# Attention: TensorE takes two key steps at a time

## The chip, the cores and the metric

The kernel runs on one core of a Trainium2 chip. What counts is the device time of one launch in microseconds (us). Three runs of the kernel before gave a median of 2147.2 us (2143.27 to 2149.08).

## The reference

One transformer block over x of shape 4 x 1024 x 512 in float32: a layer norm with scale and shift, attention with 16 heads of size 32, a gated residual, then a second norm and a mixture of 16 experts (two for each token) beside a shared feed-forward. Only the attention concerns us:

```python
kqv = (x @ Wqkv + bqkv).reshape(b, s, 3, NUM_HEADS, HEAD_SIZE)
q, k, v = kqv[:, :, 0], kqv[:, :, 1], kqv[:, :, 2]
scores = jnp.einsum('bsnh,btnh->bnst', k, q) / math.sqrt(HEAD_SIZE)
scores = jnp.triu(scores) + -10000.0 * jnp.tril(ones, k=-1)
attn = jax.nn.softmax(scores, axis=2)
out = jnp.einsum('bnkq,bknh->bqnh', attn, v)
```

The softmax runs over keys, and a query sees the keys up to itself. Each of the four batches has 1024 positions.

## The kernel before

Each engine has its own program, written out by hand, and waits on semaphores. An instruction whose semaphore is not there yet holds up everything behind it on its engine.

`attention_phase` treats a batch at a time, and in it eight pairs of heads, p = 0 to 7. A pair has 12 steps (`STEPS`): steps 0 to 7 are the eight blocks of 128 keys against the second 512 queries, steps 8 to 11 four blocks against the first 512 (`TURN` = 8 divides them). The last four steps of either part lie on the diagonal (`DIAG`) and get narrower: 512, 384, 256, 128 columns.

For each step there is:

- S, `scores` (L720): TensorE makes the scores of both heads, two matmuls from 128 x 128 weights, into one of two buffers `sc`. It waits for the exponential of two steps earlier, which frees the buffer.
- the exponential, `exp` (L445): ScalarE reads `sc` and writes one of three buffers `pr` (`PRB` = 3). It waits for the W of three steps earlier. On the diagonal GpSimd then zeroes what lies under it (L370).
- W, `weighted` (L740): TensorE multiplies `pr` with the values, and with ones for the sums. These are eight matmuls that each use 32 columns of the array, four of them side by side, and they add up in one bank `O`.

The softmax needs the maxima of each row beforehand. So while pair p is worked on, TensorE also makes plain scores of pair p + 1:

- M, `m_scores` (L695): 20 blocks for each pair (`MUSES`), one or two matmuls each, into a ring of three PSUM banks. VectorE takes the maxima from the bank (`m_reduce`, L557 and L561), and only then is the bank free. The next but two product in the ring waits for that (`bank_for`). `M_DUE` spreads the 20 blocks over the first `M_STEPS` = 9 steps, two or three to a step.
- T, `m_transpose` (L706), at step `MT_AT` = `M_STEPS` + 1: once VectorE has brought the maxima together (`m_rows`), TensorE transposes them into two ring banks, and ScalarE copies them (`mt_evac`, L434) to where the S of pair p + 1 need them.
- P, `project` (L686): in the pairs 0, 2 and 4, steps 0, 2, 4 and 6 (`P_AT`) each hold 12 matmuls that project queries or keys for later pairs. P takes a ring bank too. ScalarE and then VectorE empty it (`p_evac`, L419; `p_low`, L544).

In the pairs 2, 4 and 6 VectorE also works off eight reciprocals, one after each `m_reduce` from step 2 on (`o_recip`, L586).

The order on TensorE at a step is: S of this step, the M due, P or T if there is one, then the W of two steps earlier (`PV_LAG` = 2). ScalarE's order in a step is: exponential, `o_copy` of a finished `O` where one is due (L456, L457), `p_evac`, `mt_evac`. `o_copy` empties `O`, and the first W of the next half waits for it. Pair 7 has no M, T or P. Ahead of pair 5 ScalarE's queue also issues 12 DMAs for the next batch (`load_rows`), except in the last batch.

Of the kernel before, what the change touches and what calls it, by code (L numbers as in the profile page):

```python
# [144 lines left out]
    nc.all_engine_barrier()  # L145


M_STEPS = 9
AHEAD_V = 2
PV_LAG = 2  # L150
PRB = 3
NSLOT = 3
RPC = 4


def attention_phase(nc, K):
# [8 lines left out]
    NPAIR = H // 2  # L165
# [6 lines left out]
    TURN = 4 * CHUNKS[0] + 4  # L172
    NST = len(STEPS)
# [14 lines left out]
    NM = len(MUSES)  # L188
    M_DUE = [min(NM, -(-NM * (s + 1) // M_STEPS)) for s in range(NST)]
    MT_AT = M_STEPS + 1  # L190
    P_AT = (0, 2, 4, 6)

    NQ = 4
# [10 lines left out]
    def take(kind, kept=()):  # L204

        free = [z for z in range(3) if z not in kept]
        last = lambda z: max((n for n, at in enumerate(bank_at) if at == z), default=z - 3)
        ring.append(kind)
        bank_at.append(min(free, key=last))
        return bank_at[-1]  # L210
# [17 lines left out]
    for p in range(NPAIR - 1):  # L228
        for s in range(NST):
            for _ in range(M_DUE[s] - (M_DUE[s - 1] if s else 0)):  # L230
                take("m")
            if p % 2 == 0 and p + 2 < NPAIR and s in P_AT:
                take("p")
            if s == MT_AT:
                for _ in range(2):
# [9 lines left out]
    with ctx:  # L245
# [161 lines left out]
        def _(act):  # L407
# [14 lines left out]
            def v_evac(b, j):  # L422
                act.wait_ge(v_done, b * NT + j + 1)
                nc.scalar.activation(V[:, j * D:(j + 1) * D], bank_of("v", j)[:, :], ACT.Copy).then_inc(v_ready, 1)  # L424
# [12 lines left out]
            def exp(b, p, s):  # L437

                c, i = STEPS[s]
                off = max(0, i * P - c * CH)  # L440
                g = p * NST + s
                act.wait_ge(sc_done, b * NPAIR * NST + g + 1)
                if g >= PRB:
                    act.wait_ge(pv_done, b * NPAIR * NST + g - PRB + 1 + PRIMED)
                nc.scalar.activation(pr[:, g % PRB, :, off:], sc[g % 2][:, :, off:], ACT.Exp, scale=SCALE).then_inc(exp_done, 1)  # L445

            def o_copy(b, n):

                act.wait_ge(pv_done, b * NPAIR * NST + (n // 2) * NST + (TURN, NST)[n % 2] + PRIMED)
                p, c = n // 2, CHUNKS[n % 2]  # L450
                if p % 2 == 0 and p >= 2:
                    act.wait_ge(o_norm, b * 8 + p - 2 + n % 2 + 1 + PRIMED)
                elif p == 0:
                    act.wait_ge(o_norm, b * 8 + PRIMED)
                z = 64 * (p % 2)
                nc.scalar.activation(oT[z:z + 64, p // 2, c * CH:(c + 1) * CH], O[z:z + 64, :], ACT.Copy)  # L456
                nc.scalar.activation(oD[z:z + 64, c, :], O[64 - z:128 - z, :], ACT.Copy).then_inc(o_copied, 1)  # L457
# [23 lines left out]
            def batch(b, more):  # L481
                for j in range(AHEAD_V):
                    v_evac(b, j)
                p_evac(b, 0, range(4))
                for j in range(AHEAD_V, NT - 1):
                    v_evac(b, j)
                mt_evac(b, 0)
                v_evac(b, NT - 1)
                for p in range(NPAIR):
                    if more and p == NPAIR - 3:  # L490
                        load_rows(b + 1)
                    for s in range(NST):
                        exp(b, p, s)
                        if s == PV_LAG - 1 and p >= 1:
                            o_copy(b, 2 * p - 1)
                        if s == TURN + PV_LAG - 1:
                            o_copy(b, 2 * p)
                        if p % 2 == 0 and p + 2 < NPAIR and s in P_AT:
                            p_evac(b, (p + 2) // 2, [P_AT.index(s)])
                        if p + 1 < NPAIR and s == MT_AT:  # L500
                            mt_evac(b, p + 1)
                o_copy(b, 2 * NPAIR - 1)
                if more:
                    for j in range(NT):
                        h_evac(b + 1, bank_of("hT", j), j)
# [9 lines left out]
        def _(dve):  # L515
# [81 lines left out]
            def batch(b, more):  # L597
                p_low(b, 0, range(4))
                for n in range(NM):
                    m_reduce(b, 0, n)  # L600
                m_rows(b, 0)
                for p in range(NPAIR - 1):
                    n = r = 0
                    for s in range(NST):
                        while n < M_DUE[s]:
                            m_reduce(b, p + 1, n)
                            n += 1
                            if p % 2 == 0 and p >= 2 and s >= PV_LAG and r < 2 * RPC:
                                o_recip(b, p - 2 + r // RPC, [r % RPC])
                                r += 1  # L610
                        if p % 2 == 0 and p + 2 < NPAIR and s in P_AT:
                            p_low(b, (p + 2) // 2, [P_AT.index(s)])
                        if s == MT_AT:
                            m_rows(b, p + 1)
                if more:
                    layer_norm(b + 1)
                for n in (NPAIR - 2, NPAIR - 1):
                    o_recip(b, n, range(RPC))
                dve.wait_ge(mod2_in, b * 32 + 32)
                for j in range(NT):  # L620
                    bank = bank_of("w", j)
                    dve.wait_ge(w_done, b * NT + j + 1 + PRIMED)
                    dve.wait_ge(x1_out[j % 2], b * (NT // 2 * 16) + (j // 2) * 16 + PRIMED)
                    nc.vector.tensor_tensor(u[:, j % 2, :], bank[:, :], ga_bc[:, :], ALU.mult).then_inc(u_ready, 1)
                    if more:
                        split(b + 1, j)
# [9 lines left out]
        def _(pe):  # L636
# [27 lines left out]
            def values(b, j, between):  # L664
                pe.wait_ge(hlo_ready, b * NT + j + 1)
                bank = bank_for(b, "v", j)
                hi, lo = lambda k: hhi[:, k, j * P:(j + 1) * P], lambda k: hlo[:, j, k, :]
                terms = [(x_, w_, k) for k in range(KC) for x_, w_ in ((hi, K.whi), (hi, K.wlo), (lo, K.whi))]
                for n, (x_, w_, k) in enumerate(terms):
                    if between and n % (len(terms) // NQ) == 0:  # L670
                        between(NQ * j + n // (len(terms) // NQ))
                    last = nc.tensor.matmul(bank[:, :], x_(k), w_[:, k, 2 * D:3 * D],
                                            start=(n == 0), stop=(n == len(terms) - 1))
                last.then_inc(v_done, 1)
# [77 lines left out]
            def batch(b, more):  # L752
                def between(quarter):
                    if quarter == MT_QUARTER:
                        m_transpose(b, 0)
                    for n in first_maxima(quarter):
                        if n == 0:
                            pe.wait_ge(stk_in[0], stk_count(b, 0, 1))
                        m_scores(b, 0, n)

                for j in range(AHEAD_V):
                    values(b, j, None)
                project(b, 0, range(4))
                for j in range(AHEAD_V, NT):
                    values(b, j, between)
                for p in range(NPAIR):
                    n = 0
                    for s in range(NST):
                        scores(b, p, s)
                        if p + 1 < NPAIR:  # L770
                            if s == 0:
                                pe.wait_ge(stk_in[(p + 1) % NSLOT], stk_count(b, (p + 1) % NSLOT, p + 2))
                            while n < M_DUE[s]:
                                m_scores(b, p + 1, n)
                                n += 1
                            if p % 2 == 0 and p + 2 < NPAIR and s in P_AT:
                                project(b, (p + 2) // 2, [P_AT.index(s)])
                            if s == MT_AT:
                                m_transpose(b, p + 1)
                        g = p * NST + s - PV_LAG  # L780
                        if g >= 0:
                            weighted(b, g // NST, g % NST)
                for s in range(NST - PV_LAG, NST):
                    weighted(b, NPAIR - 1, s)
                for j in range(NT):
                    output(b, j, more)
                    if more:
                        transposes(b + 1, bank_for(b, "hT", j), j)
# [1242 lines left out]
```

## Time and profile before

| what | number |
|---|---|
| median of the runs | 2147.2 us |
| profiled execution, its own time | 2145.47 us |
| its span, first to last instruction | 2143.6 us |
| mean granted TensorE clock | 0.945 of full |
| TensorE matmul busy | 1862.2 us, 87% |
| VectorE / ScalarE / GpSimd busy | 58% / 39% / 32% |
| first S of the four batches | at 132.0, 440.0, 750.0, 1057.5 us |
| a batch's eight pairs | about 225 us, 218 in the last |

A busy time is the union of the recorded instructions of an engine. Matmuls are pipelined and overlap in the records, so the time that a group costs is read from its start to the start of the next group. A bracket behind a row gives the idle time of the engine just before it and who ended it.

### The profile page before, as it was taken

Reading aid. Unit: us, or ns where it says so; the run is one execution under the profiler, and the core shown is the slowest. Engines: PE = TensorE matmul, PEld = TensorE weight load, DVE = VectorE, ACT = ScalarE, POOL = GpSimd, SP = SyncE. Lnnn points to the kernel's source line nnn. Section 1 sums busy time; section 2 is a strip of 40 time slices with the busy share of each in tenths; the row PEclk is TensorE's granted clock in tenths of the full one; section 3 lists DMA queues with packets and bytes.
Section 4 is the critical chain, followed back from the end, with each engine's and each line's share of the span. In section 5 each row is a group of like instructions: output and inputs, shape, how many; then the busy total and the mean of one; then the engine's idle time right before and its main releaser. Section 6 shows DMA issues by size and latency. Waiting matters only on the chain. (4 is left out here: it accounts for less than half of the span.)

```text
span 2143.6 us, 34863 instructions
## 1 busy us (share of the span) xinstructions
PE 1862.2 (87%) x9947; PEld 1182.6 (55%) x9948; DVE 1245.0 (58%) x3033; ACT 845.2 (39%) x1408; POOL 675.3 (32%) x762
## 2 busy tenths in 40 slices
PE   5689989899989899899899985899999959999990
PEld 0455543555544655434554432677777747888870
DVE  3456657446667356566456644755555656675568
ACT  1325555245554245463255541222222204545541
POOL 0101115201116001125011123655554569650066
PEclk8699999999999999999999997899999979999995
DMA  5212230321232222312222305222222267754489
GB/s 199 80 32 60 60 104 30 100 56 44 51 90 65 65 60 60 75 45 69 59 60 60 79 5 193 94 94 93 90 92 87 90 222 251 247 168 150 140 323 340
DMA packets 107081, 229.60 MB, mean 107 GB/s; under 512 B 23704, under 2 KB 23704, under 8 KB 106924
## 3 DMA queue, kind: packets, MB, share of 16 engines
q1 hardware_dynamic: 81968, 166.89, 26.2%
q0 software_dynamic: 14848, 50.34, 6.9%
q10 hardware_dynamic: 10112, 10.51, 1.7%
q8 instruction: 74, 1.21, 0.2%
q14 instruction: 79, 0.65, 0.1%
HBM read 111.23 MB, written 66.12 MB: 83 GB/s over the span
## 5 line engine op out<-in xcount | busy, mean ns | idle before, releaser
L445 ACT ACTIVATE pr<-sc 128x1024 f32<-128x1024 f32 (+3 forms) x384 | 307.6, 810 | 265.8 <-PE sc L720 245.3
L370 POOL TENSOR_SCALAR_AFFINE_SELECT pr<-pr 128x256 f32<-128x256 f32 x256 | 105.1, 411 | 941.7 <-ACT pr L445 941.4
L740 PE MATMUL O<-pr,V 128*32 128x512 f32 (+3 forms) x3072 | 332.1, 507 | 14.6 <-ACT oD L457 14.4
L557 DVE CUSTOM_DVE_ANT_0 ring<-ring,mask 128x512 f32<-128x512 f32 (+3 forms) x512 | 241.8, 510 | 84.9 <-PE ring L695 82.3
L561 DVE TENSOR_REDUCE mx<-ring 128x1 f32<-128x512 f32 x256 | 170.6, 678 | 198.8 <-PE ring L695 197.0
L720 PEld LDWEIGHTS sc<-stk 128*128 128x128 f32 x768 | 116.7, 190 | 253.9 <-ACT pr L445 153.4
L720 PE MATMUL sc<-stk 128*128 128x512 f32 (+3 forms) x768 | 242.3, 398 | 13.4 <-ACT pr L445 13.4
L695 PE MATMUL ring<-stk 96*128 96x512 f32 (+3 forms) x768 | 207.3, 362 | 33.3 <-ACT V L424 13.0
L695 PEld LDWEIGHTS ring<-stk 96*128 96x128 f32 x768 | 138.8, 194 | 77.3 <-issue 22.1
L586 DVE RECIPROCAL oD<-oD 128x128 f32<-128x128 f32 x128 | 117.5, 933 | 33.2 <-ACT oD L457 33.2
L544 DVE SCALAR_TENSOR_TENSOR st<-ring,bias,st 128x512 fp32r<-128x512 f32 x64 | 48.1, 751 | 149.3 <-ACT st L419 148.8
L1793 PE MATMUL ue<-wup_e,xhi_e 128*128 x316 | 126.9, 424 | 3.8 <-DVE xlo_e L1735 3.8
L740 PEld LDWEIGHTS O<-pr,V 128*32 128x32 f32 x3072 | 62.0, 109 | 112.0 <-issue 75.9
L749 PE MATMUL ring<-wo_sb,oT 128*128 128x512 f32 x256 | 116.0, 601 | 3.1 <-POOL oT L377 3.1
L1895 POOL DMA_INDIRECT g_f<-ys,slots x64 | 70.3, 1098 | 150.5 <-POOLq L1605 131.3
L686 PE MATMUL ring<-hhi,whi 128*128 128x512 f32 x256 | 105.6, 413 | 13.2 <-DVE mx L561 12.2
L419 ACT ACTIVATE st<-ring,bias 128x512 fp32r<-128x512 f32 x64 | 44.0, 687 | 173.4 <-PE ring L686 173.4
L1176 ACT ACTIVATE relu<-up 128x512 f32<-128x512 f32 x56 | 33.5, 598 | 194.3 <-PE up L1506 194.3
L1813 PE MATMUL de<-wdn_e,ahi_e 128*128 x316 | 106.0, 417 | 0.1
L1735 DVE TENSOR_TENSOR xlo_e<-tx,xhi_e 128x512 fp32r<-128x512 f32 x79 | 54.5, 690 | 88.6 <-ACT xhi_e L1707 82.8
L686 PE MATMUL ring<-hhi,wlo 128*128 128x512 f32 x256 | 101.7, 397 | 0.0
L686 PE MATMUL ring<-hlo,whi 128*128 128x512 f32 x256 | 101.1, 395 | 0.0
(277 smaller groups left out, 3810.8 us busy)
## 6 DMA issues: line engine op xcount, KB each, us to landing
stk<-st SPq DMA_DIRECT2D x384, 128.0 KB, 2.4
x_e<-xs SPq DMA_DIRECT2D x79, 256.0 KB, 2.7
ys<-y_e SPq DMA_DIRECT2D x79, 256.0 KB, 2.1
xt<-in_L_attn_x_dram ACTq DMA_DIRECT2D x16, 512.0 KB, 6.8
st<-in_L_attn_x_dram SPq DMA_DIRECT2D x32, 256.0 KB, 2.7
x1d<-pr SPq DMA_DIRECT2D x32, 256.0 KB, 2.0
raw_e<-in_L_ffn_w_up_dram POOLq DMA_DIRECT2D x16, 512.0 KB, 5.1
raw_e<-in_L_ffn_w_down_dram POOLq DMA_DIRECT2D x16, 512.0 KB, 6.0
```

Source lines behind the costliest of these rows:

```text
L370: nc.gpsimd.affine_select(out=t, in_=t, compare_op=ALU.is_ge, fill=0.0, base=0, pattern=[[0, 2], [1, P]], channel_multiplier=-1).then_inc( ...
L445: nc.scalar.activation(pr[:, g % PRB, :, off:], sc[g % 2][:, :, off:], ACT.Exp, scale=SCALE).then_inc(exp_done, 1)
L557: last = nc.vector.tensor_tensor_reduce(out=o, in0=o, in1=K.mask[:, CH - w:CH], scale=1.0, scalar=MASKED, op0=ALU.add, op1=ALU.max, accum_ ...
L561: nc.vector.tensor_reduce(mx[:, heads[0]:heads[-1] + 1, qt, part], bank[:, 0:len(heads) * w].rearrange("p (e k) -> p e k", e=len(heads)), ...
L586: last = nc.vector.reciprocal(t, t)
L686: last = nc.tensor.matmul(bank[:, :], w_[:, k, cols], x_(k), start=(t == 0), stop=(t == len(terms) - 1))
L695: last = nc.tensor.matmul(bank[:, x_ * w:(x_ + 1) * w], K.stk[0:96, p % NSLOT, 0, e, qt * P:(qt + 1) * P], K.stk[0:96, p % NSLOT, 1, e, k0 ...
L720: last = nc.tensor.matmul(sc[g % 2][:, e, off:], K.stk[:, p % NSLOT, 1, e, i * P:(i + 1) * P], K.stk[:, p % NSLOT, 0, e, c * CH + off:(c + ...
L740: last = nc.tensor.matmul(O[row:row + 32, off:], V[:, col:col + DH], pr[:, g % PRB, e, off:], start=(i == 0), stop=(i == 4 * c + 3))
L749: last = nc.tensor.matmul(bank[:, :], oT[:, k, t * P:(t + 1) * P], K.wo[:, k, :], start=(k == 0), stop=(k == KC - 1))
L1793: both = lambda: nc.tensor.matmul(ub[s % 2][:, :], xhi[:, s % 2, k, :], part(wup, at, 2 * EI, w), start=(k == 0), stop=(k == KC - 1), skip ...
L1813: last = nc.tensor.matmul(db[s % 2][:, :], a_[:, s % 2, k, :], part(wdn, (2 * k + h) * D, D, w_down), start=(n == 0), stop=(n == len(terms ...
```

## The change

TensorE now takes the steps in twos. It issues the first S of the batch ahead of all pairs. Then, in each round of two steps (0 and 1, 2 and 3, ...), it issues the S of the second of them and the S of the step after that, the M (and P, and T) of both steps, and the W of both. `PV_LAG` is gone. ScalarE's order follows: in each round two exponentials, then `p_evac`, `mt_evac`, and the `o_copy` where a half ends. `M_STEPS` goes from 9 to 8, so the M fall due 3, 2, 3, 2, 3, 2, 3, 2 to a step, five to a round, and T comes at step 9.

```diff
-M_STEPS = 9
+M_STEPS = 8
-PV_LAG = 2
...
+                exp(b, 0, 0)
                 for p in range(NPAIR):
                     if more and p == NPAIR - 3:
                         load_rows(b + 1)
-                    for s in range(NST):
-                        exp(b, p, s)
-                        if s == PV_LAG - 1 and p >= 1:
-                            o_copy(b, 2 * p - 1)
-                        if s == TURN + PV_LAG - 1:
-                            o_copy(b, 2 * p)
+                    for s in range(0, NST, 2):
+                        exp(b, p, s + 1)
+                        if p + 1 < NPAIR or s + 2 < NST:
+                            exp(b, p + (s + 2) // NST, (s + 2) % NST)
                         if p % 2 == 0 and p + 2 < NPAIR and s in P_AT:
                             p_evac(b, (p + 2) // 2, [P_AT.index(s)])
-                        if p + 1 < NPAIR and s == MT_AT:
+                        if p + 1 < NPAIR and MT_AT in (s, s + 1):
                             mt_evac(b, p + 1)
-                o_copy(b, 2 * NPAIR - 1)
+                        if s + 2 in (TURN, NST):
+                            o_copy(b, 2 * p + (s + 2) // NST)
...
+                scores(b, 0, 0)
                 for p in range(NPAIR):
                     n = 0
-                    for s in range(NST):
-                        scores(b, p, s)
-                        if p + 1 < NPAIR:
+                    for two in range(0, NST, 2):
+                        scores(b, p, two + 1)
+                        if p + 1 < NPAIR or two + 2 < NST:
+                            scores(b, p + (two + 2) // NST, (two + 2) % NST)
+                        for s in (two, two + 1):
+                            if p + 1 == NPAIR:
+                                break
...
-                        g = p * NST + s - PV_LAG
-                        if g >= 0:
-                            weighted(b, g // NST, g % NST)
-                for s in range(NST - PV_LAG, NST):
-                    weighted(b, NPAIR - 1, s)
+                        weighted(b, p, two)
+                        weighted(b, p, two + 1)
```

## Rows read from the trace of the kernel before

**Rows 1.** Windows of pairs 2, 3, 5, 6, 7: busy (count) by engine, PEclk, DMA.

```profile
190.00:225.00 35.00, 33.27 (x200) 18.70 (x198) 22.97 (x57) 16.70 (x24) 5.74 (x10) 1.00 0.21 46
225.00:247.00 22.00, 21.26 (x156) 10.28 (x152) 13.57 (x45) 13.75 (x21) 3.28 (x8) 1.00 0.32 72
...
283.00:311.00 28.00, 23.24 (x152) 10.85 (x151) 13.56 (x45) 13.65 (x20) 3.28 (x8) 0.88 0.60 170
311.00:336.00 25.00, 22.73 (x156) 10.43 (x152) 21.12 (x57) 14.53 (x21) 5.77 (x10) 1.00 0.00 1
336.00:357.00 21.00, 18.42 (x140) 6.45 (x136) 12.18 (x24) 12.85 (x19) 11.68 (x26) 0.92 0.00 1
```

**Rows 2.** Timeline of TensorE, steps 8 to 10 of pair 1: start, length, group.

```profile
182.98 0.74 PE L720 MATMUL sc<-stk 128*128 128x512 f32 x2
183.56 0.57 PE L695 MATMUL ring<-stk 96*128 96x256 f32 x4
184.06 0.64 PE L740 MATMUL O<-pr,V 128*32 128x256 f32 x8
184.63 0.62 PE L720 MATMUL sc<-stk 128*128 128x384 f32 x2
185.18 0.43 PE L740 MATMUL O<-pr,V 128*32 128x128 f32 x8
185.53 0.51 PE L720 MATMUL sc<-stk 128*128 128x256 f32 x2
186.50 1.04 PE L706 MATMUL ring<-ident,S 128*64 128x128 f32 x8 [0.46 <-issue]
```

**Rows 3.** Timeline of TensorE, pair 2: end of a P, then W and S.

```profile
199.82 0.40 PE L686 MATMUL ring<-hlo,whi 128*128 128x512 f32 x1
200.06 0.39 PE L686 MATMUL ring<-hhi,wlo 128*128 128x512 f32 x1
200.38 1.06 PE L740 MATMUL O<-pr,V 128*32 128x512 f32 x8
201.37 0.73 PE L720 MATMUL sc<-stk 128*128 128x512 f32 x2
```

**Rows 4.** Timeline of TensorE, last batch's end: three W in a row.

```profile
1273.67 1.50 PE L740 MATMUL O<-pr,V 128*32 128x384 f32 x24
```

**Rows 5.** Timeline of all engines, start of pair 4.

```profile
247.92 0.86 PE L695 MATMUL ring<-stk 96*128 96x512 f32 x3
...
248.35 1.29 DVE L561 TENSOR_REDUCE mx<-ring 128x1 f32<-128x512 f32 x2 [4.21 <-PE ring L695]
...
249.10 0.50 PE L686 MATMUL ring<-hhi,whi 128*128 128x512 f32 x1 [0.32 <-DVE mx L561]
```

**Rows 6.** The page's costliest groups: busy, mean ns, then idle before and releaser.

```profile
L740 PE MATMUL O<-pr,V 128*32 128x512 f32 (+3 forms) x3072 | 332.1, 507 | 14.6 <-ACT oD L457 14.4
...
L686 PE MATMUL ring<-hhi,whi 128*128 128x512 f32 x256 | 105.6, 413 | 13.2 <-DVE mx L561 12.2
```

**Rows 7.** Timeline of all engines, pair 5: the last maxima and T.

```profile
305.70 0.43 DVE L557 CUSTOM_DVE_ANT_0 ring<-ring,mask 128x256 f32<-128x256 f32 x1 [0.72 <-PE ring L695]
...
308.09 1.04 PE L706 MATMUL ring<-ident,S 128*64 128x128 f32 x8 [0.46 <-issue]
```

**Rows 8.** Timeline of all engines, pair 2: what follows a P.

```profile
194.46 0.69 ACT L419 ACTIVATE st<-ring,bias 128x512 fp32r<-128x512 f32 x1 [2.78 <-PE ring L686]
...
195.18 0.75 DVE L544 SCALAR_TENSOR_TENSOR st<-ring,bias,st 128x512 fp32r<-128x512 f32 x1 [2.61 <-ACT st L419]
```

**Rows 9.** Timeline of all engines, start of pair 5 in the first batch.

```profile
289.49 1.94 ACT L445 ACTIVATE pr<-sc 128x1024 f32<-128x1024 f32 x2 [5.71 <-issue]
290.57 1.22 PE L720 MATMUL sc<-stk 128*128 128x512 f32 x2 [4.28 <-ACT pr L445]
...
295.32 0.57 PE L695 MATMUL ring<-stk 96*128 96x384 f32 x2
```

**Rows 10.** Timeline of TensorE, pair 7: the first W after the turn.

```profile
352.65 1.46 PE L740 MATMUL O<-pr,V 128*32 128x512 f32 x8 [1.41 <-ACT oD L457]
```

More of the change, by code:

```diff
@@ L190, in attention_phase @@
     MT_AT = M_STEPS + 1
+    assert MT_AT < NST - 1
     P_AT = (0, 2, 4, 6)
@@ L607, in batch @@
                             n += 1
-                            if p % 2 == 0 and p >= 2 and s >= PV_LAG and r < 2 * RPC:
+                            if p % 2 == 0 and p >= 2 and s >= 2 and r < 2 * RPC:
                                 o_recip(b, p - 2 + r // RPC, [r % RPC])
```

## The prediction

> **What bounds the kernel now.** I looked at the windows by pair first. TensorE is busy for 21.26 of 22 us in a pair without projections and for 33.27 of 35 us in one with them; VectorE for 13.57 and 22.97 us [rows 1]. So TensorE bounds those pairs. In pair 6, where the reciprocals come without projections, VectorE is busy for 21.12 of 25 us [rows 1] and sets the pace together with it. Then the timeline of TensorE: the reader is to see that S, M and W follow one another nearly without idle time, and that each takes more than its columns need [rows 2, 3]. Last, the idle times: the few that there are come from VectorE, which frees ring banks, and from ScalarE's copies of O [rows 5, 6].
>
> **What the merging saves.** From start to the next group's start a W of 128, 256 and 512 columns takes 0.35, 0.57 and 0.99 us [rows 2, 3]. That is 0.21 for each 128 columns and 0.14 that doesn't depend on them. In the row with three W in a line all 24 matmuls are done in 1.50 us [rows 4]; apart they would take 0.78 (between 0.57 and 0.99), 0.57 and, for the last, its length of 0.43: 1.78. Two merges gave 0.28, so 0.14 each. An S of 512 takes 0.58 to the next group [rows 2], though matmuls of that size in a row start 0.24 apart [rows 3], so two cost 0.47: 0.11 is paid after each W and not after another S. And W starts 0.32 after the last P matmul instead of 0.24 [rows 3]: 0.08 on entry. Together 0.33 us for each round that takes two W and two S in a row. No row shows two S in a row, so a merge is worth 0.14 at least and 0.33 at most; I take 0.33, since all three parts are rows.
>
> The Trainium skill says in "TensorEngine Tiling (Array Packing)", Key Properties, that a change of tiling mode drains TensorE; the 128-column S and M and the 32-column W are such modes. The page has no price, and the rows agree with it.
>
> There are 6 rounds in each of 32 pairs, 192 in all. In pair 6 VectorE sets the time of the first four, and in pair 7 the last two lie behind the copy that the output waits for; that leaves 192 - 16 - 8 = 168, times 0.33: **-55 us**.
>
> **What the merging costs: the ring of three banks.** A round holds five M in a row, and the fourth needs the bank of the first. The trace shows this wait where three M are followed by a P, which takes the next bank: M starts at 247.92, VectorE at 248.35 with two maxima in 1.29 us (0.65 each), and P at 249.10, 1.18 after the first M instead of 3 x 0.24 = 0.71 [rows 5]. So in the new order the fourth M starts 1.18 after the first, the fifth 0.65 later, and W another 0.32 later: 2.15 us, where five free M would take 4 x 0.24 + 0.32 = 1.28. The cost is 0.9 for each round of five M. VectorE doesn't help itself by being ahead: three maxima are left when W starts (1.95 us), and W W S S takes 2 x 0.99 - 0.22 + 0.58 + 0.47 = 2.8, so it has run dry when the next five come. W could run in that time, but it is queued behind the waiting M. This is paid in pairs 1, 3 and 5, four rounds, four batches: 48 x 0.9 = **+43 us**. Bounds: 0, if the bank always came free in time, and 1.2 each (58 us), if the fifth too waited for a full 1.18.
>
> In pairs 0, 2 and 4 the order of a round is three M, P, two M. The P now waits for the first M in all four rounds. Before it waited in the first and third; all P waits together are 12.2 us [rows 6], 1.0 a pair. The two new waits cost 1.18 - 0.71 = 0.47 each, and in pairs 2 and 4 the third gets some 0.5 longer, because a reciprocal now stands before the maxima it waits for. 12 x 0.94 + 8 x 0.5, less a little in pair 0: **+15 us** (bounds 8 and 20).
>
> **T waits longer.** From VectorE's start on the last block but one to T it takes 308.09 - 305.70 = 2.39 us [rows 7]. Before, M of step 8 was followed by T after 2.94 us [rows 2], with 0.46 idle. In the new order without P the 17th block's maxima end about 2.15 us after the first M of the round, so T comes at 4.55. TensorE is through earlier: 2.0 for its M with their waits, 0.77 for two narrow W, 0.71 for two S, 3.5 in all. So 1.05 idle instead of 0.46, **+7 us** over 12 pairs. With P, the last two M's maxima wait behind the copy and the low part of P: ScalarE starts at 194.46, when P's last matmul is through, and VectorE is done at 195.18 + 0.75 = 195.93 [rows 8], 1.47 later. A P matmul lasts 0.39 and the next group starts 0.24 after its start [rows 3], so counted from there the maxima go on at 1.47 + 0.15 = 1.6, and T comes 2.39 later, at 4.0, while TensorE has 0.5 for M, 0.85 for W W and 0.71 for S S: 2.0 idle instead of 0.46. 12 x 1.55 = **+19 us** (bounds 6 and 25).
>
> **Smaller terms.** The last W of a part comes 0.25 us too early for its triangle, since one exponential and GpSimd's work now follow S with only one W between: 28 such, **+7**. The copies of O cost TensorE 14.4 us idle in all [rows 6], 3.6 a batch, 1.41 of it at pair 7's turn [rows 10]. The first W of a pair now has two S and five M between, so that wait goes except in pair 7, where two S cover about 0.6 more of each copy: 3.6 to 1.6, **-8**. In pair 6 VectorE's work is a chain either way, and it runs dry once more, after the first five M: 1.0 a batch, **+4**. The 12 DMA issues of the next batch hold ScalarE up for 5.7 us and TensorE for 4.28 [rows 9]. They now stand behind the first exponential of the pair, so S, M and one W run beforehand; the wait falls by 1 us in three batches: **-3** (bounds -8 and +2). The stacked copies that SyncE issues come from the same P as before and have 2.5 us to spare, so I cost them at nothing.
>
> **The sum.** -55 + 43 + 15 + 7 + 19 + 7 - 8 + 4 - 3 = +29. The profiled execution took 2145.5 us (span 2143.6), 1.7 under the median of the runs. I predict 2174 us, slower by 1.4%. Nothing outside the attention changes.
>
> **Rivals.**
> 1. The merging wins. If M's waits and those of P and T were hidden, say because VectorE stays ahead or W passes the waiting M, 43 + 15 + 26 = 84 us fall away: 2174 - 84 = 2090. For it: VectorE has nearly 40% idle time in such a pair [rows 1], and the skill's drain rule alone would bring the time here. Against: the wait was there whenever the bank was needed after three M [rows 5], and TensorE's M and P are all behind semaphores in one queue. It wins from the point where these waits are under two thirds of what I worked out (55 of 84).
> 2. No difference. The waits come out at two thirds, for instance 0.5 a round instead of 0.9: 2145, within 0.3%.
> 3. The clock falls too. After 4.28 us idle in pair 5 the S of 0.73 took 1.22, and S, M, W, S took 295.32 - 290.57 = 4.75 us for what is 0.58 + 0.55 + 0.99 + 0.58 = 2.7 otherwise [rows 9, 2, 3]: the granted clock in that window was 0.88 [rows 1]. It fell after 1.41 us in pair 7 too, where a W took 1.46 [rows 10] instead of 1.06 [rows 3]. If T's new wait of 2.0 us does this in pairs 0, 2 and 4, 12 x 2.05 = 25 us come on top: 2199. Against: TensorE is dense around that wait, unlike in pair 7, and the windows with P waits stand at 1.00 [rows 1]. The Trainium skill, "TensorE: Matmul & The Clock Gate", section "A second HAM failure mode: psum-queue depth-cycling", says that short idle times between groups of matmuls that cycle through PSUM banks can make the clock toggle; by that rule the short waits at M would do it as well. The rows don't show that for waits as short as these.
>
> That the order doesn't do what it says I leave out: the code fixes TensorE's order.
>
> **Chances.** Forecast 0.66, rival 1 0.10, rival 2 0.09, rival 3 0.15. About 0.3% is what a measurement of this kernel can tell from no change. Faster 0.10, within it 0.09, slower 0.81. The range has to hold the forecast with its bounds (M 0.6 to 1.2 a round is -14 and +14) and most of rival 3: 2148 to 2204; rival 1 and a part of rival 2 are left out.
>
> **What would show it.** Right: in pairs 1 and 3 a round's five M last 2.0 us or more to W with idle time put down to L561 or L557; T idle for about 1 us, and 2 in pairs with P; two W of 512 in 1.85 us, two S of 512 in 1.05; pair 3 about 2 us longer than before, and the window of pair 7 about 2 us shorter. Wrong: no idle time at the fourth M, or a merge worth much more than 0.33. A clock below 1.00 in pairs 0 to 4 would speak for rival 3.

## The result and the profile after

| | before | after |
|---|---|---|
| median | 2145.23 us (4 runs) | 2211.32 us (4 runs, 2208.2 to 2230.92) |
| ratio | | 1.0326, 95% interval 1.0299 to 1.0352 |
| profiled execution, span | 2143.6 us | 2206.4 us |

The change makes the kernel 3.3% slower. The direction was forecast; the size wasn't: +66 us between the medians instead of +29, and outside the range of 2148 to 2204. The profiled executions agree with the medians. From a batch's first S to the first matmul of the output the four batches took 225.4, 225.3, 225.5 and 219.6 us before (the table ahead of the prediction has 218 for the last) and 241.8, 241.7, 246.1 and 234.7 after, 68 us more. What lies between and behind the batches is as it was; the stretch ahead of the first S was 5.5 us shorter in this execution, so the span grew by only 63 us.

For the first batch, stretch by stretch (from the first M of a pair to the first M of the next; starts read from TensorE's timeline, the last column by the terms of the prediction):

| stretch | before | after | change | forecast |
|---|---|---|---|---|
| first S to first M | 1.53 | 2.92 | +1.4 | 0 |
| pair 0 | 34.27 | 36.00 | +1.7 | +0.7 |
| pairs 1, 3 | 22.33 | 25.15 | +2.8 each | +2.2 |
| pairs 2, 4 | 35.4 | 36.75 | +1.35 each | +1.25 |
| pair 5 | 28.43 | 32.28 | +3.85 | +1.15 |
| pair 6, first M to T | 21.12 | 24.14 | +3.0 | +1.0 |
| T to the output | 24.54 | 22.57 | -2.0 | -2.6 |

Three of these stretches don't hold the same work before and after. Up to the first M of the batch stand two matmuls of S before and six after; pair 0 holds 80 matmuls of W before and 96 after; and pair 6 up to T holds 20 of S and 80 of W before, 16 and 64 after. Two S and two W have moved from the end of the row to its start.

The page's groups for M, P and W (columns as in [rows 6]): the idle time ahead of P that VectorE ended has gone from 12.2 us to 18.7 in its largest part alone; all idle time ahead of P has gone from 13.2 to 27.7, 14.5 more (forecast +15). W now waits for exponentials more than for the copies of O; these 14.9 us are three waits of 5.0, one in pair 5 of each batch that loads the next, where S waited before (13.4 us in three).

```profile
L740 PE MATMUL O<-pr,V 128*32 128x512 f32 (+3 forms) x3072 | 312.3, 515 | 28.4 <-ACT pr L445 14.9
...
L695 PE MATMUL ring<-stk 96*128 96x512 f32 (+3 forms) x768 | 221.8, 376 | 64.8 <-DVE mx L557 23.6
...
L686 PE MATMUL ring<-hhi,whi 128*128 128x512 f32 x256 | 106.3, 415 | 27.7 <-DVE mx L557 18.7
```

The windows of pairs 2, 3, 5, 6 and 7 (columns as in [rows 1]). Pair 6 now stands at a granted clock of 0.89 where it had 1.00, and pair 7 at 1.00 where it had 0.92.

```profile
184.00:222.00 38.00, 32.40 (x202) 19.86 (x203) 23.36 (x61) 18.39 (x27) 6.32 (x12) 1.00 0.13 30
222.00:247.00 25.00, 22.06 (x156) 11.12 (x155) 13.03 (x45) 13.23 (x19) 2.58 (x7) 1.00 0.37 83
284.00:316.00 32.00, 24.37 (x156) 11.89 (x155) 13.03 (x45) 13.20 (x19) 2.52 (x7) 0.89 0.60 163
316.00:346.00 30.00, 25.06 (x154) 11.31 (x152) 20.00 (x54) 13.87 (x21) 5.62 (x10) 0.89 0.00 1
346.00:368.00 22.00, 19.05 (x161) 7.16 (x159) 13.33 (x28) 15.62 (x24) 12.33 (x28) 1.00 0.01 2
```

TensorE's timeline in pair 1 (start, length, group). Two S of 512 take 165.42 - 164.39 = 1.03 us and two W of 512 169.48 - 167.62 = 1.86: what was forecast. The fourth M starts 1.18 after the first in the first two rounds, with VectorE named, and five M take 2.20, 2.14, 2.45 and 2.24 us to W. T has 0.74 idle ahead of it, instead of 0.46 [rows 2].

```profile
164.39 1.19 PE L720 MATMUL sc<-stk 128*128 128x512 f32 x4
165.42 0.84 PE L695 MATMUL ring<-stk 96*128 96x512 f32 x3
166.60 1.09 PE L695 MATMUL ring<-stk 96*128 96x512 f32 x2 [0.33 <-DVE mx L561]
167.62 1.92 PE L740 MATMUL O<-pr,V 128*32 128x512 f32 x16
169.48 1.20 PE L720 MATMUL sc<-stk 128*128 128x512 f32 x4
170.51 0.74 PE L695 MATMUL ring<-stk 96*128 96x512 f32 x3
171.69 1.03 PE L695 MATMUL ring<-stk 96*128 96x512 f32 x2 [0.44 <-DVE mx L561]
172.65 1.92 PE L740 MATMUL O<-pr,V 128*32 128x512 f32 x16
174.51 0.85 PE L720 MATMUL sc<-stk 128*128 128x384 f32 x4
175.20 0.88 PE L695 MATMUL ring<-stk 96*128 96x256 f32 x4
176.68 1.04 PE L695 MATMUL ring<-stk 96*128 96x128 f32 x3 [0.61 <-DVE mx L557]
177.65 1.71 PE L740 MATMUL O<-pr,V 128*32 128x512 f32 x16
...
180.08 0.75 PE L695 MATMUL ring<-stk 96*128 96x512 f32 x3
181.44 0.95 PE L695 MATMUL ring<-stk 96*128 96x256 f32 x4 [0.61 <-DVE mx L557]
182.32 0.86 PE L740 MATMUL O<-pr,V 128*32 128x256 f32 x16
...
184.70 1.04 PE L706 MATMUL ring<-ident,S 128*64 128x128 f32 x8 [0.74 <-issue]
```

In pair 2 the third and the fourth P wait 1.11 and 0.61 us, and T waits 2.07, as forecast (2.0). In the third batch the clock falls behind that wait in pairs 0 and 2: in pair 0 T and the two W behind it take 1.88 and 2.49 us (last two rows).

```profile
207.52 0.50 PE L686 MATMUL ring<-hhi,whi 128*128 128x512 f32 x1 [1.11 <-DVE mx L557]
...
214.76 0.50 PE L686 MATMUL ring<-hhi,whi 128*128 128x512 f32 x1 [0.61 <-DVE mx L557]
...
221.86 1.04 PE L706 MATMUL ring<-ident,S 128*64 128x128 f32 x8 [2.07 <-issue]
...
811.01 1.88 PE L706 MATMUL ring<-ident,S 128*64 128x128 f32 x8 [2.07 <-issue]
812.81 2.49 PE L740 MATMUL O<-pr,V 128*32 128x512 f32 x16
```

Pair 6 was not foreseen like this. The fifth M of the second round waits another 0.87 us, that of the third 0.91, since reciprocals stand between the maxima. Then two W of 512 take 3.58 instead of 1.92, and the next two 2.98 instead of 1.71: the granted clock over them is 0.53 and 0.55 of full, so they run mostly at the lower level, 1.2 GHz.

```profile
326.64 0.74 PE L695 MATMUL ring<-stk 96*128 96x512 f32 x3
327.82 0.50 PE L695 MATMUL ring<-stk 96*128 96x512 f32 x1 [0.44 <-DVE mx L561]
329.19 0.50 PE L695 MATMUL ring<-stk 96*128 96x512 f32 x1 [0.87 <-DVE mx L557]
329.62 3.58 PE L740 MATMUL O<-pr,V 128*32 128x512 f32 x16
...
336.65 0.79 PE L695 MATMUL ring<-stk 96*128 96x512 f32 x1 [0.91 <-DVE mx L561]
337.37 2.98 PE L740 MATMUL O<-pr,V 128*32 128x512 f32 x16
```

VectorE's own idle time tells what the stretch lost. From the first maximum of pair 6 to the last it was idle for 0.67 us before (at 330.51) and for 1.95 + 0.31 + 1.63 = 3.89 after: it runs dry behind the first five M, as the prediction said, but for 1.95 us instead of 1.0, and again behind each pair of slow W. In the third batch only the second pair of W is slow, and the stretch is shorter by no more than 0.5 us (23.64). The first row is of the kernel before.

```profile
330.51 0.43 DVE L557 CUSTOM_DVE_ANT_0 ring<-ring,mask 128x256 f32<-128x256 f32 x1 [0.67 <-PE ring L695]
...
327.07 0.69 DVE L561 TENSOR_REDUCE mx<-ring 128x1 f32<-128x512 f32 x1 [1.95 <-PE ring L695]
...
334.37 0.43 DVE L557 CUSTOM_DVE_ANT_0 ring<-ring,mask 128x256 f32<-128x256 f32 x1 [0.31 <-PE ring L695]
...
341.62 0.70 DVE L557 CUSTOM_DVE_ANT_0 ring<-ring,mask 128x512 f32<-128x512 f32 x1 [1.63 <-PE ring L695]
```

In pair 5 the 12 DMA issues begin at 288.50, when the copies of O are on their way, and the second exponential follows at 296.43; the W that needs it has waited 4.97 us, and works at the lower clock (1.94 instead of 1.07). At the batch's start the third S waits 1.26 for the first exponential, ahead of all M. The first row is again of the kernel before, where the first M waited 0.90.

```profile
133.58 0.94 PE L695 MATMUL ring<-stk 96*128 96x512 f32 x3 [0.90 <-ACT V L424]
...
128.85 0.74 PE L720 MATMUL sc<-stk 128*128 128x512 f32 x2 [1.26 <-ACT pr L445]
...
297.51 1.94 PE L740 MATMUL O<-pr,V 128*32 128x512 f32 x8 [4.97 <-ACT pr L445]
```

ScalarE's timeline at the same place:

```profile
288.35 0.59 ACT L456 ACTIVATE oT<-O 64x512 f32<-64x512 f32 x1
288.50 0.37 ACTq L464 DMA_DIRECT2D mod_t<-modd  x1
288.95 0.60 ACT L457 ACTIVATE oD<-O 64x512 f32<-64x512 f32 x1
289.03 4.29 ACTq L464 DMA_DIRECT2D mod_t<-modd  x7
293.50 2.76 ACTq L467 DMA_DIRECT2D xt<-in_L_attn_x_dram  x4
296.43 1.94 ACT L445 ACTIVATE pr<-sc 128x1024 f32<-128x1024 f32 x2 [6.88 <-issue]
```

### The profile page after: what moved, and what is told of

It reads as the page before. It is cut to its first block and busy times, and to the rows that moved or that the text cites. A ratio compares the mean times of both kernels' runs of the same rounds, so it can differ in the third digit from the quotient of the medians.

```text
span 2206.4 us, 34863 instructions
## 1 busy us (share of the span) xinstructions
PE 1847.6 (84%) x9947; PEld 1197.7 (54%) x9948; DVE 1240.1 (56%) x3033; ACT 836.6 (38%) x1408; POOL 674.2 (31%) x762
## 3 DMA queue, kind: packets, MB, share of 16 engines
q1 hardware_dynamic: 81968, 166.89, 25.4%
## 5 line engine op out<-in xcount | busy, mean ns | idle before, releaser
L445 ACT ACTIVATE pr<-sc 128x1024 f32<-128x1024 f32 (+3 forms) x384 | 295.2, 809 | 288.2 <-PE sc L720 259.7
L740 PE MATMUL O<-pr,V 128*32 128x512 f32 (+3 forms) x3072 | 312.3, 515 | 28.4 <-ACT pr L445 14.9
L695 PE MATMUL ring<-stk 96*128 96x512 f32 (+3 forms) x768 | 221.8, 376 | 64.8 <-DVE mx L557 23.6
L720 PE MATMUL sc<-stk 128*128 128x512 f32 (+3 forms) x768 | 197.1, 378 | 5.0 <-ACT pr L445 5.0
L720 PEld LDWEIGHTS sc<-stk 128*128 128x128 f32 x768 | 121.2, 192 | 126.6 <-issue 98.0
L740 PEld LDWEIGHTS O<-pr,V 128*32 128x32 f32 x3072 | 76.7, 111 | 184.8 <-issue 109.0
L686 PE MATMUL ring<-hhi,whi 128*128 128x512 f32 x256 | 106.3, 415 | 27.7 <-DVE mx L557 18.7
```

The costliest lines, as they stand in the source:

```text
L686: last = nc.tensor.matmul(bank[:, :], w_[:, k, cols], x_(k), start=(t == 0), stop=(t == len(terms) - 1))
L695: last = nc.tensor.matmul(bank[:, x_ * w:(x_ + 1) * w], K.stk[0:96, p % NSLOT, 0, e, qt * P:(qt + 1) * P], K.stk[0:96, p % NSLOT, 1, e, k0 ...
L720: last = nc.tensor.matmul(sc[g % 2][:, e, off:], K.stk[:, p % NSLOT, 1, e, i * P:(i + 1) * P], K.stk[:, p % NSLOT, 0, e, c * CH + off:(c + ...
L740: last = nc.tensor.matmul(O[row:row + 32, off:], V[:, col:col + DH], pr[:, g % PRB, e, off:], start=(i == 0), stop=(i == 4 * c + 3))
```

## The experiments

Two theories stood against each other. The ring theory: five M in a row wait for VectorE to empty one of three banks, and that costs more than the merging saves. The order theory: grouping S and W is itself the loss, through their waits for exponentials and copies. Ratios are to the kernel before, measured beside each run. Between them stand the odd terms: ScalarE's DMA issues and pair 6.

**v_short.** The changed kernel, with VectorE's part made short.

```diff
-o = bank[:, x_ * w:(x_ + 1) * w]
+o = bank[:, (x_ + 1) * w - P:(x_ + 1) * w]
...
-bank[:, 0:len(heads) * w].rearrange("p (e k) -> p e k", e=len(heads)),
+bank[:, 0:len(heads) * P].rearrange("p (e k) -> p e k", e=len(heads)),
```

> The changed kernel, but VectorE takes each maximum over 128 columns only (of the block's columns the first 128, or the 128 on the diagonal), so each ring bank comes free earlier; the order on TensorE is that of the changed kernel. The maxima are then not those of whole rows. Ring theory: the waits at M, at P and at T shrink to a third or less, pairs 1 and 3 fall from 25.15 to about 21 us, and the time is about 2135. Order theory: VectorE's time doesn't matter and it stays within 10 us of 2211.

Measured: 2128.24 us, ratio 0.9922 (0.9905 to 0.9938): 83 us under the changed kernel with the same order on TensorE. In its timeline of pair 1 the waits in the first two rounds are gone, and five M take 1.43 and 1.56 us to W; in the other two rounds 0.35 and 0.21 us of waits are left.

```profile
166.83 1.51 PE L695 MATMUL ring<-stk 96*128 96x512 f32 x5
168.26 1.92 PE L740 MATMUL O<-pr,V 128*32 128x512 f32 x16
...
171.13 1.62 PE L695 MATMUL ring<-stk 96*128 96x512 f32 x5
172.69 1.92 PE L740 MATMUL O<-pr,V 128*32 128x512 f32 x16
```

So VectorE's time is what the new order waits for. But pairs 1 and 3 only fell to 22.55 us, not to 21, and so stay above the 22.33 of before: in pair 1 T still has 0.51 us idle, the M 0.57, and the last W waits 0.58 for its triangle from GpSimd. Such waits take a good part of the merging's gain.

**b_burst5.** One part of the change alone: five M at once, in the order of before.

```diff
-M_DUE = [min(NM, -(-NM * (s + 1) // M_STEPS)) for s in range(NST)]
+M_DUE = [min(NM, 5 * (s // 2 + 1)) for s in range(NST)]
```

> The order of before, but M due five at each even step and none at the odd ones, so the five M in a row are there and the merged S and W are not. Ring theory (the fourth and fifth M wait for VectorE to free one of three banks): the fourth M starts 1.18 us after the first, a round of five costs 0.9 to 1.1 more, pairs 1 and 3 go from 22.3 to about 25.9 us from M to M, and the time is about 2195. Order theory (the loss comes from grouping S and W, with their waits for ScalarE): pairs 1 and 3 stay at 22.3 and the time at 2145.

Measured: 2304.2 us, ratio 1.0735 (1.0717 to 1.0752). Pairs 1 and 3 took 26.2 us (expected 25.9), and the fourth M stands 172.16 to 173.35, 1.19 us behind the first, without any merging. The total was 109 us higher than I expected, mostly because in pairs 2 and 4 (42 to 47 us) P comes behind all five M and VectorE's reciprocals, and the clock falls on P (0.63 a matmul instead of 0.40).

```profile
172.16 0.86 PE L695 MATMUL ring<-stk 96*128 96x512 f32 x3
173.35 1.09 PE L695 MATMUL ring<-stk 96*128 96x512 f32 x2 [0.32 <-DVE mx L561]
```

**c_two_parts.** The merges kept, the five M split around the two S. Here two M and P came first.

```diff
-M_DUE = [min(NM, -(-NM * (s + 1) // M_STEPS)) for s in range(NST)]
+M_DUE = [min(NM, 5 * (s // 2) + (2, 5)[s % 2]) for s in range(NST)]
...
-scores(b, p, two + 1)
-if p + 1 < NPAIR or two + 2 < NST:
-    scores(b, p + (two + 2) // NST, (two + 2) % NST)
 for s in (two, two + 1):
+    if s > two:
+        scores(b, p, two + 1)
+        if p + 1 < NPAIR or two + 2 < NST:
+            scores(b, p + (two + 2) // NST, (two + 2) % NST)
...
```

> The changed kernel, but each round's five M stand in two parts: two M (and P) ahead of the two S, three behind them. S and M use the array in the same mode, so both merges stay and no more than three M follow one another. Ring theory: the waits at the fourth M go, pairs 1 and 3 fall from 25.15 to about 21 us, pair 6 loses its two falls of the clock, and the time is about 2120, under the kernel before. Order theory: within 10 us of the changed kernel's 2211.

Measured: 2302.47 us, ratio 1.0725 (1.0707 to 1.0743), 182 us above what I expected. The pairs that the experiment was meant for did what the ring theory said, pairs 1 and 3 at 22.0 us, under the 22.33 of before. The pairs with P went to 45 to 49 us, and the row says why: with this place the last M of a round needs the bank that P holds, and ScalarE, then VectorE, empty it behind two exponentials whose S come after P.

```profile
210.82 0.50 PE L695 MATMUL ring<-stk 96*128 96x512 f32 x1 [2.46 <-DVE st L544]
```

**c2_two_parts.** The same with P behind the third M.

```diff
-M_DUE = [min(NM, -(-NM * (s + 1) // M_STEPS)) for s in range(NST)]
+M_DUE = [min(NM, 5 * (s // 2) + (3, 5)[s % 2]) for s in range(NST)]
...
+while p + 1 < NPAIR and n < M_DUE[two] - 1:
+    m_scores(b, p + 1, n)
+    n += 1
 scores(b, p, two + 1)
```

> Again the changed kernel with each round's five M in two parts, two ahead of the two S and three behind, but P now behind the third M, as in the changed kernel, so that no M of the round needs the bank that P holds. Ring theory: pairs 1 and 3 at 22.0 us as in the first such run, pairs 2 and 4 at about 34 us instead of 36.75 (their P no longer wait at M, T still does), pair 6 about 22.3 from M to T, and the time about 2128. Order theory: pairs 2 and 4 stay at 36.7 or more.

Measured: 2145.88 us, ratio 1.0001 (0.9987 to 1.0015): 65 us under the changed kernel with both merges in place, no difference to before, and 18 above what I expected. Pairs 1 and 3 stand at 22.0 and pair 6 at 22.1, as expected; the first M follows the first S after 1.53 us again, since it stands ahead of the next two S. In the first batch's pair 6 the clock still falls for one pair of W (2.80 us instead of 1.71), yet the stretch is 2.0 us shorter than in the changed kernel. Pairs 2 and 4 are at 36.4 mostly and 34.8 in the rest. The P no longer wait at three of the four places, but T's 2.07 us stays, and here the clock falls behind it in 8 of the 12 pairs with P: two W take 2.95 instead of 1.71.

```profile
219.56 1.43 PE L706 MATMUL ring<-ident,S 128*64 128x128 f32 x8 [2.07 <-issue]
220.91 2.95 PE L740 MATMUL O<-pr,V 128*32 128x512 f32 x16
```

**d_spread** and **b_spread.** The 12 DMA issues of `load_rows` taken apart, in the changed kernel and in the one before (there one issue behind each exponential).

```diff
-if more and p == NPAIR - 3:
-    load_rows(b + 1)
...
+if more and p == NPAIR - 3:
+    load_rows(b + 1, (s, s + 1))
```

> The changed kernel with load_rows taken apart: two of the 12 DMA issues in each round of pair 5 instead of all 12 ahead of its second exponential. If ScalarE's queue is what holds pair 5 up, the 5 us wait of a W in pair 5 goes, pair 5 falls from 32.3 to about 25.2 us in three batches, and the time is about 2190. If the DMAs themselves (their traffic) hold it up, pair 5 stays at 32 us and the time at 2211.

> The kernel before with its load_rows taken apart, one DMA issue behind each exponential of pair 5. ScalarE's queue theory: pair 5 goes from 28.4 to 22.4 us in three batches and the time from 2144 to about 2126. If the DMAs hold it up by their traffic: no change.

Measured: 2184.82 us, ratio 1.019 (1.0155 to 1.0225), and 2127.16, ratio 0.9915 (0.9891 to 0.994). Pair 5 goes to 25.15 us in all batches, as pairs 1 and 3, and to 22.3 in the kernel before. So ScalarE's queue is the cause, and by the medians load_rows costs 26 us in the changed kernel and 17 in the one before. The intervals of the two ratios are some 8 and 5 us wide to either side; pair 5 alone, in the profiles, has 23 and 18. In the changed kernel the W in question has no wait ahead of it:

```profile
291.38 1.92 PE L744 MATMUL O<-pr,V 128*32 128x512 f32 x16
```

**k_recip.** The reciprocals made nearly free.

```diff
+t = t[:, 0:1]
 last = nc.vector.reciprocal(t, t)
```

> The changed kernel with each reciprocal taken over 1 of its 128 columns, so VectorE's reciprocals are nearly free (the other columns stay undivided). If pair 6 lost its 3 us because the reciprocals stand between the five maxima that TensorE's M wait for, and TensorE then idles until its clock falls, pair 6 goes from 24.15 us from first M to T to about 19.3, as in pairs 1 and 3, its two half-clock stretches go, pairs 2 and 4 lose the third P's longer wait (0.6), and the time is about 2187 instead of 2211. If pair 6 lost them to the order alone (exponentials, copies), it stays at 24.

Measured: 2196.99 us, ratio 1.0245 (1.0228 to 1.0262). Pair 6 took 19.4 us to T, and its window stands at a clock of 1.00 (0.89 in the changed kernel): the reciprocals between the maxima are what its TensorE waited for, and without those waits the clock didn't fall. Since the run takes VectorE's work away as well, it doesn't part the cost of the waits from that of the clock. Of the 24 us that I expected 14 came, because other stretches grew: pair 5 took 33.7 instead of 32.3 us and pair 0 37.5 instead of 36.0, with half-clock stretches that stand elsewhere now.

```profile
333.22 1.09 PE L696 MATMUL ring<-stk 96*128 96x512 f32 x2 [0.44 <-DVE mx L561]
334.24 1.92 PE L741 MATMUL O<-pr,V 128*32 128x512 f32 x16
```

**f_plan, g1_plan, g2_plan.** A version that mends what was found. A function `plan` writes down, for each pair and round, which M and P go ahead of the two S and which behind; the ring, TensorE and VectorE follow it. With P it is two M, S S, one M, P, two M; in the last such round P comes behind all M, and VectorE brings the maxima together before it takes up P. Without P it is three and three in f_plan, two and three in g1_plan. load_rows is spread in all. g2_plan moves ScalarE's copies of T's second half behind the exponentials of the last round. The lines below are those of g1_plan and g2_plan.

```diff
+for r, (a, z) in enumerate(((2, 3),) * 4):
+    m = [("m", x) for x in range(n, n + a + z)]
+    n += a + z
+    tail = m[a:]
+    if with_p:
+        at = 1 if r < 3 else len(tail)
+        tail = tail[:at] + [("p", r)] + tail[at:]
+    out.append((m[:a], tail))
```

> The changed order with three things mended: M in two parts around the two S (three and three in the pairs without P, and all 20 done by the first part of the fourth round; two and three with P), the last P behind all M and the maxima brought together ahead of its low part, and load_rows spread over pair 5. Ring theory, with T's wait going too: pairs 1 and 3 at about 21.3 us, pairs 2 and 4 at about 32.5, pair 5 as pair 3, pair 6 about 22, the time about 2080 and so 3% under the kernel before. Order theory: not under 2144.

> As f_plan, but with two and three M around the two S in all pairs, so six in a round no longer meet VectorE's pace. Pairs 1 and 3 from 22.66 to 22.0 us or less, pair 6 from 24.75 to about 22.2, pairs 2 and 4 at 34.5, the time about 2115. If the M's waits in f_plan were not from six in a round, it stays at 2129.

> As g1_plan, with ScalarE's copies of the second half of T's bank moved behind the two exponentials of the last round (1.2 us earlier exponential of step 11). If the last W of a pair waits for its triangle because those copies stand ahead of its exponential, that wait (0.43 to 0.8 us a pair) goes and the time is about 2098, 17 under g1_plan. If the wait has another cause, no difference between the two.

Measured: f_plan 2129.48 us, ratio 0.992 (0.99 to 0.9939), 49 us above what I expected; pairs 1 and 3 took 22.66 (two of the eight 23.7) and pair 6 24.75 (one of the four 25.4), since six M a round are again too many. g1_plan 2114.11 us, ratio 0.9859 (0.9839 to 0.9878), with pairs 1, 3 and 5 at 22.0 in nine of twelve places (23.5 in the others), pairs 2 and 4 at 34.5 to 35.0 and pair 6 mostly at 22.2: expected 2115. It beats both kernels, and b_spread too, though by only some 13 us: that is what the new order brings over the old one when both have load_rows spread. g2_plan 2118.66, ratio 0.9884 (0.9867 to 0.99), where I expected 2098: the wait of the last W did go (pairs 1, 3 and 5 at 21.56), but the stretch from the last T to the output took 23.4 instead of 22.5 us, and the times of the two don't differ by more than their intervals.

## Why the prediction was right in its direction and wrong in its size

- **What the merging saves, 0.33 a round: right for a round, not for the time.** Two S and two W in a row cost what the sum had. But six rounds of 0.33 should take 2.0 us off a pair, and the shortest pairs 1 and 3 of any run, those of g2_plan, are 0.8 us under the 22.33 of before; new waits took most of the rest (TensorE idles 1.7 us in such a pair, 0.7 before). The last pair, which has no M, became 2.0 us shorter, but that isn't the merging alone: there the waits for copies of O fell from 2.6 to 0.8 us, and 1.5 us of waits for triangles came.
- **The ring of three banks, +43: right in cause, a little small in size.** The fourth M stands 1.18 us behind the first in the changed kernel and 1.19 in b_burst5, where nothing else was changed. Five M took 9.03 us in the four rounds of pair 1; I had 4 x 2.15 = 8.6. v_short shows that VectorE's time is what they wait for, c2_two_parts that the wait goes when the burst is halved and the merges stay. The order theory fell as the account of the 66 us.
- **P and T: right.** The third and fourth P of pair 2 wait 1.11 and 0.61 us, where the one of [rows 5] waits 0.32, and T has 2.07 us idle with P and 0.74 without; I had 2.0 and 1.05 from [rows 7, 8]. Pairs 2 and 4 came within 0.1 us of the forecast.
- **Smaller terms: this is the step that failed.** The load was put at -3 us: "so S, M and one W run beforehand; the wait falls by 1 us in three batches". They do run beforehand, but on ScalarE the issues now stand behind the copies of O that wait for the last W of the pair before, and from the first issue (288.50) to the next exponential (296.43) it is 7.9 us; TensorE waits 4.97 us where it waited 4.28 [rows 9]. So the load costs more than before, not less: 5 us by pair 5 in the profiles, 9 by the medians of the two spread runs, instead of -3. Pair 6 was put at +1 a batch, as a chain of VectorE's that "runs dry once more". It took +3, 12 us instead of 4: VectorE ran dry for 1.95 us instead of 1.0, and again behind W that the lower clock made slow.
- **Left out altogether: the S and W that moved ahead.** The three S ahead of the first M add 1.4 us a batch, 1.03 of it for two S and the rest for a longer wait (1.26 us, where the first M waited 0.90 before), and pair 0, with two narrow W more, took 1.0 more than forecast. The same S and W left pair 6's stretch, where they saved nothing, since VectorE sets its time. That is 2.4 a batch, some 10 us in all.
- **Also small:** the last W's wait for its triangle, 0.25 in the sum, is worth about 0.44 where no P follows: pairs 1 and 3 go from 22.0 us in g1_plan to 21.56 in g2_plan, which removes it. That is 0.2 more than forecast and the M of pair 1 took 0.4 more, while T's wait was 0.3 shorter; so 0.3 of the 0.6 by which pairs 1 and 3 are longer than forecast is accounted for, and the rest is not. Over the whole run the waits for triangles are 10.3 us (7 forecast), and those for copies of O fell from 14.4 to 3.2 (8 less forecast).
- **Rival 3, the clock: in the wrong place.** It does fall, and costs, but behind T's 2.07 us in only two of 12 pairs of the changed kernel's profile, where I had put it, and in pair 6 in every batch, where I hadn't. In c2_two_parts the same 2.07 us is followed by a fall in 8 of 12, in d_spread in 4. What decides it beyond the length of the wait stays open.

Added up for the first batch: 16.4 us instead of 7.2. Of the 9.2 between them 2.7 are pair 5, 2.0 pair 6, 1.4 the start, 1.3 pairs 1 and 3, 1.0 pair 0, and 0.8 the rest. The third batch lost some 4 us more to the clock. That pairs 2 and 4 and the ring came out close doesn't make the total right: the missed terms nearly all lie on the same side, so they add up.

## What to carry to other kernels

Before work is grouped to save switches on one engine, count how many buffers each burst takes and how fast they come back: here a burst of five products into three banks cost about 1.0 us a round (26.2 us for a pair's four rounds in b_burst5 instead of 22.3), and taking S and W in twos saved 0.33. Products that share a mode can stand on both sides of the group (two M, S S, three M), which keeps the merge and halves the burst. Work that is moved out of a stretch which another engine paces saves nothing there, and costs its time where it goes. And an engine's DMA issues count as its work: moved behind a wait, they start later by that wait.

## What the runs showed of the hardware

- Going from the 128-column products to the 32-column ones and back cost TensorE about 0.33 us: two W of 512 in a row took 1.86 us instead of 2 x 0.99, two S 1.03 instead of 2 x 0.58, and 0.08 is paid on entry [rows 3].
- One DMA issue on ScalarE's queue took 0.6 to 0.7 us (7 in 4.29, 4 in 2.76), and the next activation waited behind all of them.
- The same idle time of 2.07 us ahead of T was followed by the full clock in pair 2 of one kernel (T 1.04) and by the lower one in another (T 1.43, then two W in 2.95), so the length of that one wait doesn't foretell it.
